# Attention inside one core: VectorE's score pairs move into ScalarE's score buffers, and two accumulators take turns

## What is computed

```python
x = L0_attn_query; xn = _layernorm(x, axis=-1)
q = _split_heads(xn @ q_w.T + q_b, 16) / 4.0;  k, v = the same with k_w, v_w
scores = jnp.einsum('bhqd,bhkd->bhqk', q, k)          # per head 4096 x 4096
attn = jax.nn.softmax(scores, axis=-1)
ctx = jnp.einsum('bhqk,bhkd->bhqd', attn, v)          # back to 4096 x 256
x = x + (ctx @ out_w.T + out_b) + ffn(xn)             # ffn: one fp8-quantised 256 x 256 matmul
```

## Time and profile before

| | |
|---|---|
| time, median of 3 runs | 1961.22 us (1954.82 to 1961.71) |
| the profiled execution | 1961.78 us, its span 1960.0 us |
| busy over the span | PE 98%, ACT 92%, DVE 65%, POOL 2% |
| exponentials on ScalarE | 1920 of 128x1024 |
| granted TensorE clock, mean | 0.992 |

### The profile page before, as it was taken

One profiled execution on the slowest core, in us unless ns is written; L12 is line 12 of the kernel. 1 busy time (PEld: TensorE's weight loads), 2 busy tenths in 40 slices (PEclk: granted clock), 3 DMA queues, 4 the chain that ended last, 5 costly groups with the idle time before them and its releaser, 6 DMA issues.

```text
span 1960.0 us, 39423 instructions
## 1 busy us (share of the span) xinstructions
PE 1912.2 (98%) x14963; PEld 687.3 (35%) x14963; DVE 1274.3 (65%) x1789; ACT 1812.5 (92%) x1993; POOL 44.2 (2%) x53
## 2 busy tenths in 40 slices
PE   5969999999999999999999999999999999999998
PEld 3623333333333333333333333333333333333337
DVE  6645765756566765756566765756566666656567
ACT  2339999999999999999999999999999999999991
POOL 2000000000000000000000000000000000000000
PEclk9979999999999999999999999999999999999999
DMA  7880111203021121203011121203011121203014
GB/s 198 270 250 3 25 31 26 31 10 47 9 34 15 25 31 26 31 10 47 10 31 18 25 31 26 31 10 47 9 27 22 25 31 26 31 10 47 10 21 109
DMA packets 65632, 83.87 MB, mean 43 GB/s; under 512 B 9952, under 2 KB 47360, under 8 KB 62208
## 3 DMA queue, kind: packets, MB, share of 16 engines
q1 hardware_dynamic: 65472, 81.58, 20.4%
HBM read 54.79 MB, written 26.21 MB: 41 GB/s over the span
## 4 chain that ended last, share of the span: by engine, by line
PE 93%; SPq 2%; DMA 1%; DVE 1%; ACT 1%; issue 1%; ACTq 0%
PE banks L1121 48%; PE banks L1100 36%; PE banks L1128 3%; PE banks L1011 2%; PE banks L1232 1%; PE banks L1022 1%; DVE o_sb L824 1%; ACT probs L608 1%; DMA k_parts<-probs 1%; PE banks L1058 1%; PE banks L1078 0%; DMA q_st<-q_parts 0%; PE banks L1216 0%; SPq L305 0%; PE banks L1224 0%
## 5 line engine op out<-in xcount | busy, mean ns | idle before, releaser
L608 ACT ACTIVATE probs<-banks 128x1024 f32<-128x1024 f32 x1920 | 1769.6, 1162 | 11.0 <-PE banks L1100 5.7
L1121 PE MATMUL banks<-probs,v_st 128*32 128x512 f32 x7680 | 1026.9, 607 | 5.6 <-DVE o_sb L824 5.4
L1100 PE MATMUL banks<-q_st,k_st 50*128 50x512 f32 x4096 | 814.4, 457 | 5.3 <-ACT probs L608 4.3
L1100 PEld LDWEIGHTS banks<-q_st,k_st 50*128 50x128 f32 x4096 | 361.2, 184 | 698.3 <-ACT probs L608 629.1
L856 DVE SCALAR_TENSOR_TENSOR horner<-horner,bits 128x1024 f32<-128x1024 f32 x256 | 313.6, 1225 | 8.8
L843 DVE TENSOR_SCALAR bits<-banks 128x512 int32<-128x512 f32 x256 | 176.9, 691 | 135.0 <-PE banks L1100 119.1
L1121 PEld LDWEIGHTS banks<-probs,v_st 128*32 128x32 f32 x7680 | 151.3, 108 | 321.1 <-issue 203.4
L824 DVE STREAM_TRANSPOSE o_sb<-banks 128x512 f32<-128x512 f32 x32 | 22.9, 717 | 311.6 <-PE banks L1121 311.6
L861 DVE SCALAR_TENSOR_TENSOR d_probs<-horner,powers 128x1024 f32<-128x1024 f32 x128 | 156.8, 1225 | 97.8 <-PE banks L1128 94.5
L852 DVE SCALAR_TENSOR_TENSOR horner<-bits 128x1024 f32<-128x1024 f32 x128 | 156.9, 1226 | 4.4
L1128 PEld LDWEIGHTS banks<-d_probs,v_st 128*32 128x32 f32 x2048 | 66.6, 110 | 153.2 <-issue 153.2
(11 more groups left out here) (90 smaller groups left out, 450.1 us busy)
## 6 DMA issues: line engine op xcount, KB each, us to landing
k_st<-k_parts SPq DMA_DIRECT2D x204, 128.0 KB, 4.4
q_st<-q_parts SPq DMA_DIRECT2D x204, 64.0 KB, 4.6
q_parts<-probs SPq DMA_DIRECT2D x9, 512.0 KB, 6.3
k_parts<-probs SPq DMA_DIRECT2D x9, 512.0 KB, 6.5
xnT_copy<-probs SPq DMA_DIRECT2D x8, 512.0 KB, 4.4
probs<-xnT_copy SPq DMA_DIRECT2D x8, 512.0 KB, 6.7
w_f<-xnT_copy SPq DMA_DIRECT2D x16, 256.0 KB, 5.3
out_dram<-horner SPq DMA_DIRECT2D x16, 256.0 KB, 2.1
```

The costliest lines, as they stand in the source:

```text
L608: act.activation(probs[:, at:at + WIDE * CHUNK].rearrange("p (t c) -> p t c", t=WIDE), banks[:, bank:bank + WIDE, :], ACT.Exp, scale=1.0 / ...
L1100: return pe.matmul(out, k_mm[rows, kt * P:(kt + 1) * P], blocks[rows, qb // GROUPS], start=True, stop=True)
L1121: last = pe.matmul(banks[VCOLS * qb:VCOLS * (qb + 1), 6, :], v_st[:, kt, :], probs[:, at:at + CHUNK], start=first_one, stop=last_one, tile ...
```

## The change

- **Pairs.** VectorE now takes 5 whole pairs a unit (`D_PAIRS`: both pairs of row 15, both of row 31, one of row 30) out of the same three buffers that ScalarE uses, at places 9, 21, 31, 41 and 51 (`D_AT`) of the unit's 64. `buffer_free` waits for `d_taken` where the pair three places back was VectorE's. ScalarE has 59 pairs a unit. The first instruction of `d_block` reads two banks (128 x 1024) at once.
- **Rounds.** A unit is 32 rounds of two pairs of scores and one whole sum; round r scores pairs 2r + 3 and 2r + 4 and sums the row at index r - 1 of `SUM_ROWS`. The odd places of `D_AT` are the first pair of their round. There are no single tiles and no pieces of sums.
- **Accumulators.** Unit u sums in bank 6 + u. The sampled maxima are made in the other unit's bank, in rounds 6 and 7 (`MAX_ROUNDS`), between the round's two pairs.
- **Maxima.** VectorE transposes `neg` itself (32 x 32 blocks, a 128 x 32 tile) into `neg_row`; TensorE's transpose and `turn_maxima` are gone. `load_rows` issues 16 DMAs instead of 4.
- **Loads.** The first 128 keys get a load and semaphore of their own (`k_first`, 6 more DMAs a head, and 6 more at the start); k's first half is loaded after its last read.
- **VectorE's heads** are written out instead of looped.

```diff
-    D_ROWS = (KT // 2 - 1, KT - 1)
-    D_SLOTS = ((2, 4, 6, 14), (16, 24, 34, 36))
-    D_SUM = ((27, 29, 31, 33), (49, 51, 53, 55))
-    MAX_SLOTS, MAX_TURN = (38, 40), 46
+    D_AT = (9, 21, 31, 41, 51)
+    D_PAIRS = ((KT // 2 - 1, 0), (KT // 2 - 1, 1), (KT - 1, 0), (KT - 1, 1), (KT - 2, 0))
+    MAX_ROUNDS = (6, 7)
...
+        SUM_ROWS = []
+        for s_at in range(KT):
+            left = [kt for kt in range(KT) if kt not in SUM_ROWS]
+            SUM_ROWS.append(min(left, key=lambda kt: max(PLACE[kt, j] + (12 if (kt, j) in D_PAIRS else 0)
+                                                         for j in range(QB // WIDE))))
...
             def load_rows(c, u, count):
                 sp.wait_ge(c.row_ready, count)
                 for i in range(PARTS):
                     for g in range(GROUPS):
...
+                        for b in range(BLOCKS):
+                            first_row = b * PARTS * UT + r0
+                            sp.dma_start(to[:, b], neg_row[first_row:first_row + GT, :]).then_inc(c.row_in[u], 16)
...
             sp.wait_ge(consts, 9)
+            load_k(first, 0, 2)
             load_k(first, 0, 0)
...
+                    dve.wait_ge(c.st_done, h * HP + (pair + 1))
+                    dve.tensor_scalar(words.rearrange("p (t c) -> p t c", t=WIDE), banks[:, bank:bank + WIDE, :],
+                                      -EXP_BIAS, EXP_BIAS, ALU.max, ALU.add).then_inc(c.d_taken, 1)
...
+                    if n >= 2:
+                        dve.wait_ge(c.pv_done, h * STEPS + (PV_0 + u * KT + SUM_AT[D_PAIRS[n - 2][0]] + 1))
...
+                def head_sampled(h):
+                    lk = h * HEAD_LINKS + c.links_0
+                    for u in range(UNITS):
+                        for n in range(D_BLOCKS):
+                            d_block(h, u, n)
+                            if n == 0:
+                                maxima(h * UNITS + (u + 1), 1 - u, lk)
+                        if u:
+                            quantise_part(h)
+                        sums(h, u, lk + MAX_LINKS)
...
+                    back, m = divmod(n - BUFS, HP)
+                    u, p = divmod(m, PAIRS)
+                    if p in D_AT:
+                        pe.wait_ge(c.d_taken, h * HD + (D_0 + back * HD + u * D_BLOCKS + D_AT.index(p) + 1))
+                    else:
+                        pe.wait_ge(c.exp_done, h * HE + (EXP_0 + back * HE + u * AE + A_INDEX[p] + 1))
...
+                def sampled_heads():
+
+                    for r in range(HEADS * HP // 2):
+                        nxt = [divmod(n, HP) for n in (2 * r + LEAD, 2 * r + LEAD + 1) if n < HEADS * HP]
+                        for h, n in nxt:
+                            arrivals(h, n)
+                        for i, (h, n) in enumerate(nxt):
+                            scores(h, n)
+                            u, at = r // (PAIRS // 2), r % (PAIRS // 2)
+                            if i == 0 and at in MAX_ROUNDS:
+                                sampled_maxima(u // UNITS, u % UNITS, MAX_ROUNDS.index(at))
+                        if r:
+                            unit, at = divmod(r - 1, KT)
+                            weighted_sum(unit // UNITS, unit % UNITS, at)
+                    weighted_sum(HEADS - 1, UNITS - 1, KT - 1)
```

More of the change, by code:

```diff
@@ L252, in program @@
         ACC_0 = 1
+        D_0 = 1
         OUT_0 = 16
@@ L269, in saved_in_half_1 @@
             return SAVED_0 + (32 * (NCH // 2) if i < 4 else 0) + 16 * uses
[L271 to L279, removed]
-        WHOLE = [(i, d) for _, i, d, piece, _ in SUM_ORDER if piece in (None, D_PIECES - 1)]
@@ L281, in program @@
[L281 to L291 removed]
+        ORDER = []
@@ new lines, in program @@
+        for kt in range(KT):
+            for j in range(QB // WIDE):
+                if (kt, j) not in D_PAIRS:
+                    if len(ORDER) in D_AT:
+                        ORDER.append(D_PAIRS[D_AT.index(len(ORDER))])
+                    ORDER.append((kt, j))
+        PLACE = {pair: p for p, pair in enumerate(ORDER)}
+        A_PLACES = [p for p in range(PAIRS) if p not in D_AT]
+        A_INDEX = {p: a for a, p in enumerate(A_PLACES)}
+        FROM_HALF_1 = min(p for p, (kt, j) in enumerate(ORDER) if kt >= KT // 2)
@@ L293, in program, with sums_before_reuse, span @@
+        SUMMED = [1 + max(SUM_AT[kt] for kt in range(half * (KT // 2), (half + 1) * (KT // 2))) for half in range(2)]
+        def sums_before_reuse(a):
+            before, a = divmod(a - SLOTS, HE)
+            u, a = divmod(a, AE)
+            return before * STEPS + u * KT + SUM_AT[ORDER[A_PLACES[a]][0]] + 1
+        def span(start, count):
+            return slice(start, start + count) if isinstance(start, int) else bass.ds(start, count)
         tok = "(t p) d -> p t d"
@@ new lines, in head_full @@
+                def head_full(h):
+                    lk = h * HEAD_LINKS
+                    jobs = h * (UNITS * c.max_jobs)
+                    maxima(jobs, 0, lk)
+                    for n in range(D_BLOCKS):
+                        d_block(h, 0, n)
+                    maxima(jobs + c.max_jobs, 1, lk + MAX_LINKS)
+                    sums(h, 0, lk + 2 * MAX_LINKS)
+                    for n in range(D_BLOCKS):
+                        d_block(h, 1, n)
+                    sums(h, 1, lk + (2 * MAX_LINKS + SUM_LINKS))
@@ L937, in outputs @@
+                if c.full:
+                    with dve.Fori(0, HEADS) as h:
+                        head_full(h)
+                else:
+                    for h in range(HEADS):
+                        head_sampled(h)
+                dve.wait_ge(c.chain, HEADS * HEAD_LINKS + c.links_0)
             def outputs(again):
@@ new lines, in scores @@
+                def scores(h, n):
+                    u, p = divmod(n, PAIRS)
+                    kt, j = ORDER[p]
+                    bank = WIDE * ((n if c.full else h * HP + n) % BUFS)
+                    blocks = q_mm[:, u * UG:(u + 1) * UG].rearrange("k (c j x) -> k j c x", j=QB // GROUPS, x=P)
+                    buffer_free(h, n)
+                    for g in range(GROUPS):
+                        rows = slice(g * GROUP, g * GROUP + STACK)
+                        last = pe.matmul(banks[:, bank + g, :], k_mm[rows, kt * P:(kt + 1) * P], blocks[rows, j],
+                                         start=True, stop=True)
+                    last.then_inc(c.st_done, 1)
```

443 lines of the change are left out of this document (194 added, 249 removed).

## The result

The changed kernel takes 1978.31 us (median of 4 runs, 1976.90 to 1978.88) against 1959.77 us for the kernel before (4 runs, 1954.82 to 1961.71): a ratio of 1.0097, with a 95% interval of 1.0077 to 1.0118. It is slower by some 19 us; 1981.5 was forecast. The profiled execution took 1978.53 us, its span 1976.7.

The account below looks back on a forecast made before the run. ScalarE was taken as the bound: a unit 54.10 + 1.65 = 55.75 us against 55.28, 15 us over 32 units. With the prologue, 1961.8 + 5.5 + 15 = 1982.3 profiled, so 1981.5 us forecast, its own range 1971 to 1994.

Parts of the forecast that it names:

- The bound, and ScalarE's rate: In the heads ScalarE is the bound, one exponential per 0.917 us, 55.02 of a unit's 55.28 us before.
- The Trainium skill's rule: Lighten the engine with the highest occupancy: 32 exponentials taken from ScalarE are worth 32 x 0.917 = 29 us.
- What a VectorE pair does: ScalarE loses 0.30 us behind every VectorE pair, plus 0.17 at the maxima: 1.65 us a unit.
- the rival of hidden pairs: Buffers hide VectorE pairs in the heads, ScalarE's 54.10 us a unit stand: 1929.5 us; chance 0.11.
- The ledger's check: The same ledger of waits, run for the order of before with single tiles and pieces, gives 55.3 us a unit.
- TensorE's total of before, 54.9 us: TensorE's work per unit in the kernel before: rounds, VectorE row pieces, single tiles and maxima, 54.9 us.
- VectorE: In the heads: first step 1.23 us, blocks about 7.8 us, pairs at least 8.5 apart, so VectorE is in time.
- Loads in the heads: q for unit 1's maxima lands in time, by 3 to 4 us; a later landing would stall TensorE once a head.
- The prologue: Row loads in SyncE's queue delay the awaited save; heads start 5.5 us later, bounds 2 and 9 us.
- The low clock: Loss to the low clock at the start of the heads left as it is, give or take 1 us.

Follow-up runs that it names:

- run 5: Changed kernel, all sums but a unit's first and last in two halves, the second between the next round's two pairs of scores: 2220.76 and 2222.02 us.
- run 1: Changed kernel with VectorE's pairs one place later (10, 22, 32, 42, 52), second in their rounds: 1985.87 us, ratio 1.0124 to the kernel before.
- run 2: Changed kernel with VectorE's second to fifth pair one round later (9, 23, 33, 43, 53): 1975.31 us, ratio 1.0069 to the kernel before.
- run 3: Changed kernel with four VectorE pairs a unit instead of five (9, 21, 31, 41): 1998.62 us, ratio 1.0192 to the kernel before.
- run 4: Changed kernel, columns 256 to 511 of the sum left out in the five rounds that score a VectorE pair: 1942.52 us, ratio 0.9911 to the kernel before.
- run 12: Kernel before with three constants changed, moving single tiles, maxima with their transpose, and pieces of row 31: 1960.15 us, ratio 0.9989 to the kernel before.
- run 6: Changed kernel with six VectorE pairs, the sixth at place 61: 2057.95 us, ratio 1.0492 to the kernel before.
- run 7: Changed kernel with one accumulator, bank 6 for both units and the maxima in bank 7: 1977.19 us, ratio 1.0093 to the kernel before.
- run 11: Changed kernel, pairs at 9, 23, 33, 43, 53, prologue's row loads on GpSimd's queue ahead of its reduction, k's first half loaded in one piece: 1967.35 us.
- run 10: Changed kernel with the prologue's 16 row loads on GpSimd's queue ahead of its reduction: 1975.38 us, ratio 1.0073 to the kernel before.
- run 9: Changed kernel with the prologue's 16 row loads on GpSimd's queue behind its reduction: 1983.03 us, ratio 1.0116 to the kernel before.
- run 8: Changed kernel with the prologue's 16 row loads issued after the last save: 1983.50 us, ratio 1.0115 to the kernel before.

## Why the prediction held, step by step

**The bound, and ScalarE's rate.** Right: 0.917 us by the ends of the records, in all runs but run 5, where TensorE set 0.993. The Trainium skill's rule (Perfetto Trace Analysis, Identifying the Most-Contended Engine), which gave 1929.5 by the rival, did not pay here: the engine with most to do lost 32 exponentials, and a unit went from 55.30 to 55.73.

**What a VectorE pair does.** Right in place and size: forecast 0.30 us behind each and 0.17 for the maxima, 1.65 us a unit; measured 0.30 and 0.17, 1.67. Runs 1 to 3 bear out place, debt and size, and run 4 takes half of the sum away and with it the wait. A unit was forecast at 55.75 and is 55.73. The 55.28 that it was set against counts the last unit, which is shorter (54.6); counted like the rest it is 55.30, so a unit grew by 0.43 and not by 0.47. The point from which the rival of hidden pairs decides, 0.17 us a pair, was not near.

**The ledger's check.** The prediction trusted its ledger of waits because it gave 55.3 us for the order of before. That agreement was weaker than it seemed: for the same order with three constants moved (run 12) the ledger gave 55.09 and the unit stayed at 55.30. For the kernel after and runs 1 to 3 it was right to 0.02 us.

**TensorE's total of before, 54.9 us.** Nothing in the sum came from it, and it holds two errors that offset. More of the same chain of the kernel before, start us, us:

```profile
1028.88 0.89 PE banks L1100 x5
1029.77 1.00 PE banks L1121 x8
1030.77 0.89 PE banks L1100 x4
...
1069.35 0.42 PE banks L1100 x2
1069.77 0.26 PE banks L1078
1070.03 0.43 PE banks L1100 x2
```

A single tile was given 0.34 us, from 1059.12 to 1061.12; but in most rounds the scores with a single tile take 0.89, so 0.23 for the tile, 8 x 0.11 = 0.9 us less. The transposition of the maxima was left out: its round has 0.42 + 0.26 + 0.43 us in place of 0.66, so 0.45 more. That makes 54.4 to 54.5, with both engines below the period of 55.30. Moving three constants (run 12) did not win the rest.

**VectorE.** Right: first step 1225 ns for 1.23, the maxima's small transposition 0.21 us within the bounds, idle before its blocks, and in the heads no wait of TensorE for it but one of 0.2 us. Run 6 shows how near the end is: a pair at 61, whose row is the last sum, comes too late.

**Loads in the heads.** Right: the wait for q before the maxima's scores (L1078) occurs once, 8.2 us at the start, and in no head.

**The prologue.** Mechanism right, size too small: 8.0 us for the 5.5 forecast, inside the bounds of 2 to 9. The 16 loads were issued from 123.54 and not from 119.9, since the saves before them were not all issued by then, and took 11.09 us, within the 10.2 to 11.7. Only a small part was there earlier: TensorE's second group of the prologue (L1020; L995 in the kernel before) starts at 28.39 us instead of 27.00, which the change does not touch. In runs 6 and 7 it starts at 27.0 as before, and their first exponentials still come at 141.40 and 140.81. So some 7 us belong to the change. The term that was mis-sized is that of the six more k loads, taken at 0.5 to 1 us as hidden behind the transfers: SyncE issues k's first loads for 5.45 us instead of 2.67, all that stands behind them comes later, and run 11, which drops them, begins some 2 us earlier than run 10 for it. The transfers, expected to be bound by bandwidth here, pause instead while SyncE issues rows. The window from 131.6 to 135.2 us of the kernel after, columns as in the earlier trace rows, has a DMA share of 0.02 and 2 GB/s, where the kernel before had 1.02 over the whole stretch from 120 to 134:

```profile
131.60:135.20 3.60, 0.77 (x2) 0.00 (x0) 2.09 (x5) 0.69 (x1) 0.47 (x2) 1.00 0.02 2
```

**The low clock** was taken as unchanged, give or take 1 us; it gave 4.5 us back. That is the largest error of the sum. Against the forecast for the profiled execution, 1982.3, the terms are +2.5 in the prologue, -4.5 here, -0.6 in the output stage and -1.2 in the units (0.43 us each for 0.47): -3.8, and 1978.53 is 3.8 below. That the first two partly offset each other is luck, and makes the total look better than its terms.

## What to carry to other kernels

Before work is taken from the busiest engine, follow one round through the buffers that it shares with an engine that works in order. Here three buffers and a whole sum between two scores return only 0.62 of each 0.917 us; in the kernel before, where VectorE's tiles were scored beside the buffers, all waits of a unit came to some 0.28 us. One exponential of 60 less made a unit 0.8% longer, and the same gap behind every VectorE pair was the sign. The Trainium skill (Perfetto Trace Analysis, Optimization Strategy) takes regular bubbles as a hint at too few buffers, and the trace agrees as far as 0.30 us behind each of 160 pairs goes; a fourth buffer was not tried.

Sixteen small DMAs ahead of a large one that is awaited hold it back: 11.09 us of issue, and some 4 us of the start of the heads. Moved to another engine's queue ahead of its next wait (run 10) they cost little; behind that wait (run 9) the heads began later than with them in place, at 145.90 instead of 141.94.

## What the runs showed of the hardware

- ScalarE's records hide waits: 0.19 us idle is shown where 0.30 us is lost, for the records become shorter behind a wait and longer in a row. Only ends can be subtracted.
- By difference, each stretch of one kind of matmul pays 0.14 to 0.18 us once: one pair of scores between sums takes 0.42 us and two in a row 0.66; a sum of half the columns takes 0.57 us and the whole 1.00 (run 5).
- GpSimd issues the same 16 row loads in 8.55 us for which SyncE needs 11.09.
- The granted clock of 0.5 at the start of the heads lasted from 10.2 us (run 10) over 13.7 (after) and 17.0 (before) to 20.5 us (runs 8 and 9) in these kernels, and how much of it lies behind the first exponential changes the time by several us without any change in the work.
